# Edge sums with groups dealt out by cost, the look of the next turn ahead, and slice tokens two windows deep

## The reference, cut to what matters

```
x = x + relation_conv(ln(x))        # 8 relations, segment sum over dst
x = x + gat_gated_experts(ln(x))    # attention over 131072 edges gates 4 experts
x = x + sage(ln(x), src, dst)       # below
x = x + slice_attention(ln(x))      # below

# sage
h_sparse = maxk(feat @ W_neigh, 32)
summed = segment_sum(h_sparse[src], dst)
out = feat @ W_self + summed / max(deg, 1)

# slice attention, 8 heads x 64 slices
w = softmax((x_mid @ W_slice + b_slice) / temp)      # per node and head
slice_token = einsum(fx_mid, w) / (w.sum(nodes) + 1e-5)
```

## Time and profile before

| | us |
|---|---|
| median of 3 runs | 5771.85 (5771.05 to 5776.82) |
| the profiled execution | 5768.18 |
| its span | 5766.4 |

### The profile page before, as it was taken

The page is one execution under the profiler, slowest core; times in us unless marked ns, Lnnn a source line. Parts: engine busy times, 40 slices in busy tenths (PEclk is TensorE's granted clock), DMA queues, the critical chain, the costliest instruction groups (busy, mean ns, idle before and its releaser), DMA issues. The chain is left out here.

```text
span 5766.4 us, 72842 instructions
## 1 busy us (share of the span) xinstructions
PE 4709.5 (82%) x18114; PEld 2969.5 (51%) x18115; DVE 2677.6 (46%) x9248; ACT 1130.5 (20%) x2248; POOL 3249.8 (56%) x3351
## 2 busy tenths in 40 slices
PE   3998887888788888824999999957688999984888
PEld 1553333333333333313777777744466788852446
DVE  6562333333333222242555555557866555634442
ACT  1331000000000000002444444434211111100222
POOL 1114777777777777711777777722477766670001
PEclk9997566666666655555999999979899999986998
DMA  3333333333334333312323233342455544431001
GB/s 133 131 124 127 105 105 105 105 105 105 105 105 112 105 105 105 105 29 45 60 59 59 59 59 59 60 143 99 131 161 155 147 132 132 129 107 24 0 0 45
DMA packets 312422, 545.12 MB, mean 95 GB/s; under 512 B 74736, under 2 KB 212735, under 8 KB 305811
## 3 DMA queue, kind: packets, MB, share of 16 engines
q0 software_dynamic: 141088, 319.86, 21.4%
q1 hardware_dynamic: 171092, 222.51, 12.0%
HBM read 449.02 MB, written 93.08 MB: 94 GB/s over the span
## 5 line engine op out<-in xcount | busy, mean ns | idle before, releaser
L959 PE MATMUL e_sums<-e_ring,e_onehot 128*128 128x257 f32 x3136 | 1621.6, 626 | 345.1 <-DMA e_ring<-table,erow 260.5
L713 POOL DMA_INDIRECT e_ring<-table,erow x1568 | 1490.6, 951 | 477.9 <-issue 360.0
L959 PEld LDWEIGHTS e_sums<-e_ring,e_onehot 128*128 128x128 f32 x3136 | 722.5, 281 | 1239.1 <-issue 908.3
L1878 POOL DMA_INDIRECT t_source<-source_rows,t_index x848 | 809.7, 955 | 281.3 <-issue 230.9
L1049 POOL DMA_INDIRECT e_ring<-table,esrc x800 | 789.4, 987 | 311.0 <-PE e_sums L1136 158.0
L914 DVE SCALAR_TENSOR_TENSOR big<-e_sums,within,big 128x257 f32 x196 | 95.0, 485 | 1286.4 <-PE e_sums L959 1286.4
L1136 PE MATMUL e_sums<-e_ring,e_onehot 128*128 128x256 f32 x1600 | 484.2, 411 | 112.2 <-DMA e_ring<-table,esrc 91.8
L1122 PE MATMUL e_total<-e_loads,e_times 128*128 128x256 f32 x2176 | 538.2, 382 | 0.0
L2027 PE MATMUL t_raw<-big,t_w 128*128 (+1 forms) x1600 | 441.3, 438 | 1.3
L1122 PEld LDWEIGHTS e_total<-e_loads,e_times 128*128 128x128 f32 x2176 | 399.7, 191 | 65.2
L1136 PEld LDWEIGHTS e_sums<-e_ring,e_onehot 128*128 128x128 f32 x1600 | 298.9, 199 | 237.0 <-DVE e_onehot L1091 103.6
(11 more groups left out here) (383 smaller groups left out, 5214.8 us busy)
## 6 DMA issues: line engine op xcount, KB each, us to landing
table<-r_stage SPq DMA_DIRECT2D x49, 1024.0 KB
e_loads<-table SPq DMA_DIRECT2D x384, 128.0 KB
t_near<-near_rows SPq DMA_DIRECT2D x106, 256.0 KB
e_ring<-table,erow POOLq DMA_INDIRECT x1568, 2.7
m_outputs<-first_outputs SPq DMA_DIRECT2D x49, 512.0 KB, 4.6
first_outputs<-t_stage SPq DMA_DIRECT2D x96, 256.0 KB
t_source<-source_rows,t_index POOLq DMA_INDIRECT x848, 2.4
e_ring<-table,esrc POOLq DMA_INDIRECT x800, 3.1
```

The lines of the kernel that those rows point to most:

```text
L713: eng.indirect_dma_start(ring[:, t % BODY, 0:D], None, table, bass.IndirectOffsetOnAxis(ap=b.erow[:, t:t + 1], axis=0)).then_inc(gathered[ ...
L959: eng.matmul(sums[g % SUMS][:, 0:ACCW], onehot[t % ONEHOTS][:, :], ring[:, t % BODY, :], start=(t % GROUP == 0), stop=(t % GROUP == GROUP ...
L1878: eng.indirect_dma_start(source[s][:, q, :], None, a.source_rows, bass.IndirectOffsetOnAxis(ap=index[s][:, q:q + 1], axis=0)).then_inc(gat ...
```

## The change

Six things change. **Neighbour sums**: (1) a group's place among the tiles follows from a cost of 3 + 4 x width, dealt over 784 tiles; (2) the row marks are made by ScalarE as Relu(1 - |source - column|), two Abs and one Relu per group, two groups ahead of the copy; (3) the totals lie in two sets of PSUM banks, two windows to a bank, cleared by matmuls with zeros, and a block's totals are taken in after six groups of the next block. **Attention edges**: (4) `look` of turn t+1 stands behind `hide` of turn t, so `columns` is called for two turns in a body. **Slice tokens**: (5) the bias matmul goes; `blogit` is made on all 128 partitions and VectorE adds it, PSUM to SBUF, ahead of the maximum; (6) GpSimd normalises the rows, into four buffers instead of two; turning is parted from scoring and stands two windows ahead; the loop is written out. The diff, cut:

```diff
 neighbour_sums
-    BODIES = (NT - FROM) // BODY
-    BEGIN = [sum(DGROUPS // n for n in DSTEPS[0:i]) for i in range(DENSE + 1)]
+    LATER = 6
+    TILES = NT - FROM
+    GROUPS = DENSE * DGROUPS
+    COST = [3 + 4 * wide(g) for g in range(GROUPS)]
+    tile_of = [sum(COST[0:g]) * (TILES - BODY) // sum(COST) for g in range(GROUPS)]
+    groups_at = [[] for _ in range(TILES)]
+    for g, at in enumerate(tile_of):
+        groups_at[at].append(g)
...
-        row = [sb(f"e2_row{s}", [P, P], BF16) for s in range(MARKS)]
+        zeros = sb("e2_zeros", [P, BANK], BF16)
+        away = [sb(f"e2_away{s}", [P, 2, P]) for s in range(2)]
+        row = [sb(f"e2_row{s}", [P, 2, P], BF16) for s in range(MARKS // 2)]
...
-        total = [ctx.enter_context(nc.psum_tensor(f"e2_total{k}", [P, BANK], F32)) for k in range(DWIDE)]
+        total = [ctx.enter_context(nc.psum_tensor(f"e2_total{s}", [P, DWIDE, D], F32)) for s in range(2)]
...
 scalar
+            def mark(g):
+                s = g % 2
+                wait_if(eng, rowed, g - 1)
+                for two in range(2):
+                    c = column(2 * g + two)
+                    eng.activation(away[s][:, two, :], b.ramp[:, 0:P], ACT.Abs, bias=b.dsrc[:, c:c + 1],
+                                   scale=-1.0).then_inc(parted, 1)
+                wait_if(eng, tallied, g - MARKS // 2 + 1)
+                eng.wait_ge(parted, 2 * (g + 1))
+                eng.activation(row[g % (MARKS // 2)][:, :, :], away[s][:, :, :], ACT.Relu, bias=b.ones[:, 0:1],
+                               scale=-1.0).then_inc(rowed, 1)
...
+            mark(0)
+            mark(1)
+            for g in range(GROUPS):
+                if g + 2 < GROUPS:
+                    mark(g + 2)
+                copy(g)
...
 vector, mark
-                    eng.tensor_scalar(row[q][:, :], rampn[:, :], b.dsrc[:, column(tile):column(tile) + 1], None,
-                                      ALU.is_equal).then_inc(marked, 1)
...
 vector, order
+                for g in groups_at[t]:
+                    mark(g)
+                    if g % DGROUPS == LATER and g > DGROUPS:
+                        take(block(g) - 1)
+                if t % GROUP == 4 and t // GROUP >= 1:
+                    add(t // GROUP - 1)
+            add(TILES // GROUP - 1)
+            take(DENSE - 1)
...
 tensor, inner
+                if g % DGROUPS == 0:
+                    wait_if(eng, taken, BEFORE[max(n - 1, 0)])
+                    for q in range(0, DWINDOWS[n], 2):
+                        eng.matmul(into[:, q:q + 2, :].rearrange("p w d -> p (w d)"), zeros[:, 0:P], zeros[:, :],
+                                   start=True, stop=False, skip_group_check=True)
...
 attention_edges, tensor
             def body(t, s, w, e):
-                column = columns(t)
-                look(t, s, column)
                 if e is not None:
                     hide(t, w, e)
+                if not last_turn(t, 1):
+                    look(t + 1, 1 - s, columns(t + 1))
                 if e is not None and not first_turn(t, 1) or isinstance(t, int) and t == UNITS:
                     project(t - 1, 1 - s, e - 1 if e else EXPERTS - 1)
-                total(t, s, column)
+                total(t, s, columns(t))
...
 slice_weights, tensor
-                eng.matmul(bias[0:1, h * SG:(h + 1) * SG], bx[:, h:h + 1], wslice[:, :], start=True, stop=False)
-                mm = eng.matmul(bias[0:1, h * SG:(h + 1) * SG], one[:, :], bslice[:, :], start=False, stop=True)
+                eng.matmul(bias[:, h * SG:(h + 1) * SG], bx[:, h:h + 1].broadcast_to([SD, P]), wslice[:, :], start=True, stop=False)
+                mm = eng.matmul(bias[:, h * SG:(h + 1) * SG], b.ones[0:1, :], bslice[:, :], start=False, stop=True)
...
 slice_tokens
+        @block.gpsimd
+        def _(eng):
+            for s in range(XNS):
+                eng.memset(xn[s][:, D:ACCW], 1.0).then_inc(ones, 1)
+            for w in range(NW):
+                wait_if(eng, summed, w - XNS + 1)
+                eng.tensor_scalar(xn[w % XNS][:, 0:D], b.x[:, w, :], b.mean[:, w:w + 1], b.rstd[:, w:w + 1],
+                                  ALU.subtract, ALU.mult).then_inc(normed, 1)
...
 vector, lower
-                eng.tensor_reduce(top[s][:, :], by_head(logits[s][:, :]), AX_X, ALU.max).then_inc(topped, 1)
+                eng.tensor_tensor(biased[s][:, :], logits[s][:, :], f.blogit[:, :], ALU.add).then_inc(topped, 1)
+                eng.wait_ge(topped, 2 * w + 1)
+                eng.tensor_reduce(top[s][:, :], by_head(biased[s][:, :]), AX_X, ALU.max).then_inc(topped, 1)
...
 scalar
+            copy(0, 0)
+            copy(1, 1)
+            grow(0, 0)
+            for w in range(NW):
+                if w + 2 < NW:
+                    copy(w + 2, w % 2)
+                keep(w)
+                if w + 1 < NW:
+                    grow(w + 1, (w + 1) % 2)
...
 tensor
-                eng.matmul(logits[s][:, :], b.ones[0:1, :], f.blogit[:, :], start=False, stop=True).then_inc(scored, 1)
...
+            turn(0, 0)
+            turn(1, 1)
             score(0, 0)
+            for w in range(NW):
+                if w + 1 < NW:
+                    score(w + 1, (w + 1) % 2)
+                if w + 2 < NW:
+                    turn(w + 2, w % 2)
+                tokens(w, w % 2, LAST if w == NW - 1 else P)
```

More of the change, by code:

```diff
@@ L1029, in _, with copy @@
             for s in range(AHEAD):
-                eng.wait_ge(fetched[s], 16 * (DENSE * DGROUPS // AHEAD))
-        @block.scalar
+                eng.wait_ge(fetched[s], 16 * (GROUPS // AHEAD))
+        @block_ctx.scalar
         def _(eng):
-            for g in range(DENSE * DGROUPS):
+            def mark(g):
[9 more added lines that the diff above has]
+                               scale=-1.0).then_inc(rowed, 1)
+            def copy(g):
                 n = wide(g) * P
@@ L1038, in _ @@
                 eng.activation(times[g % TIMES][:, 0:n], tally[g % 2][:, 0:n], ACT.Copy).then_inc(copied, 1)
-        @block.gpsimd
+            mark(0)
+            mark(1)
+            for g in range(GROUPS):
+                if g + 2 < GROUPS:
+                    mark(g + 2)
+                copy(g)
+        @block_ctx.gpsimd
         def _(eng):
@@ L1100, in _ @@
-            add(BODIES * BODY // GROUP - 1, 1)
-            eng.wait_ge(added, 2 * (BODIES * BODY // GROUP))
-            eng.wait_ge(taken, BEFORE[DENSE])
-        @block.tensor
+                if a.n:
+                    a.settled()
+                if k.n:
+                    k.settled()
+                for q in range(DWINDOWS[n]):
+                    window = b.accs[:, bass.ds(w + q, 1), 0:D].rearrange("p a c -> p (a c)")
+                    k.did(eng.tensor_tensor(window, window, total[n % 2][:, q, :], ALU.add))
@@ L1107, in outer @@
                 wait_if(eng, copied, g - 1)
+                eng.wait_ge(rowed, g + 1)
+                eng.wait_ge(marked, 2 * (g + 1))
                 for two in range(2):
-                    q = (2 * g + two) % MARKS
-                    eng.wait_ge(marked, 2 * (2 * g + two + 1))
-                    mm = eng.matmul(tally[g % 2][:, 0:wide(g) * P], row[q][:, :], place[q][:, 0:wide(g) * P],
+                    mm = eng.matmul(tally[g % 2][:, 0:wide(g) * P], row[g % (MARKS // 2)][:, two, :],
+                                    place[(2 * g + two) % MARKS][:, 0:wide(g) * P],
                                     start=(two == 0), stop=(two == 1))
@@ L1119, in inner @@
                 eng.wait_ge(copied, g + 1)
                 eng.wait_ge(fetched[g % AHEAD], 16 * (g // AHEAD + 1))
-                for k in range(DWINDOWS[n]):
-                    mm = eng.matmul(total[k][:, 0:D], times[g % TIMES][:, k * P:(k + 1) * P], loads[:, g % AHEAD, :],
-                                    start=(r == 0), stop=(r == DGROUPS - 1))
+                for q in range(DWINDOWS[n]):
+                    mm = eng.matmul(into[:, q, :], times[g % TIMES][:, q * P:(q + 1) * P], loads[:, g % AHEAD, :],
+                                    start=False, stop=False, skip_group_check=True)
@@ L1124, in inner @@
                 mm.then_inc(spread, 1)
[L1126 to L1142 removed]
+            eng.wait_ge(numbered, 2)
@@ new lines, in _ @@
+            for t in range(TILES):
+                s, g8 = t % BODY, t // GROUP
+                if t % GROUP == 0:
+                    wait_if(eng, added, 2 * (g8 - 1))
+                eng.wait_ge(matched, t + 1)
+                eng.wait_ge(gathered[s], 16 * (t // BODY + 1))
+                eng.matmul(sums[g8 % 2][:, 0:D], onehot[t % ONEHOTS][:, :], ring[:, s, :],
+                           start=(t % GROUP == 0), stop=(t % GROUP == GROUP - 1)).then_inc(summed, 1)
+                for g in groups_at[t]:
+                    outer(g)
+                    if g > 1:
+                        inner(g - 2)
+                    if g == GROUPS - 1:
+                        inner(g - 1)
+                        inner(g)
@@ L2056, in _ @@
```

(2 more changed lines are left out.)

172 lines of the change are left out of this document (55 added, 117 removed).

## The result

The changed kernel takes 5589.66 us (median of 4 runs, 5585.27 to 5592.74), the kernel before 5771.76 beside it: a ratio of 0.9682, 95% interval 0.9665 to 0.9699. The forecast was 5598, in a range of 5550 to 5660. The profiled execution took 5587.87 us, its span 5586.1, against 5766.4.

A forecast was written before the change was run, and what follows sets the result against it. GpSimd and, in wide blocks, TensorE bound neighbour sums; GpSimd bounds attention edges; a circle of waits bounds slice tokens. Gains 55 + 8 + 110 = 173 us gave 5598 us, own range 5565 to 5630, with rivals A and B 5550 to 5660.

The forecast's parts named there:

- The dealt groups: Neighbour sums: dealing groups by cost moves the bound from TensorE to GpSimd; gathers 1042 us against 1099, net 55 gained.
- The stretch: Neighbour sums, wide blocks: GpSimd's issue lengthened beside VectorE's wide marks, 0.18 us per group, giving 1.318 us per tile.
- stand closer without the row marks between them: Neighbour sums, a bound: marks of a burst closer together, stretch 0.14 per tile, about 24 us gained.
- Rival A: Neighbour sums: the stretch vanishes with the row marks, GpSimd keeps 1.25 us; 42 us more gained, 5556; chance 0.13.
- rival B: Slice tokens: each window's subtraction or product waits out a whole GpSimd normalisation, 1.22 us; 59 us, so 5657; chance 0.14.
- Row marks on ScalarE: Neighbour sums: two Abs and one Relu per group fit on ScalarE, 1.1 to 1.4 us with the copy; cost taken as nothing.
- Rival D: Neighbour sums: Abs or Relu needs another function table, two loads per group; stage 1410 us, kernel 5966; chance 0.02.
- 8 of the 19 us: Attention edges: the earlier look removes part of GpSimd's waits for VectorE; 8 us taken from a span of 0 to 19.
- rival C: Attention edges: the second column load is not hidden and TensorE's turn grows; 5646; chance 0.09.
- the period 4.6: Slice tokens: a window takes 4.6 us instead of 7.0, from VectorE's chain of 4.58; net 110 gained, bounds 85 to 121.
- TensorE's work was taken as 4.5: Slice tokens: TensorE's own work per window, scores, turning, flips and tokens, 4.5 us together, nearly tying with VectorE's chain.

The follow-up runs named there:

- rows_on_vector: The changed kernel with the row marks of the neighbour sums made by VectorE again, all else kept: 5563.39 us, ratio 0.9639 to the kernel before.
- deep_rows: The changed kernel with row marks back on VectorE and slice tokens' lowering and scoring one window deeper: 5554.3 us, ratio 0.9615 to the kernel before.
- load_twice: The kernel of look_back with the column offsets loaded a second time ahead of the totals: 5608.24 us, ratio 0.9701 to the kernel before.
- look_back: The changed kernel with the look of turn t back ahead of its hidden layer and one offsets load per turn: 5610.16 us, ratio 0.9704.

## Why the prediction was right

**The dealt groups: right in its mechanism.** With the old places the gathers took 1098.4 us, 53 more than the changed kernel's 1045.4. That TensorE stops being the bound and GpSimd is late next is what the idle time before the gathers says.

**The stretch: the size nearly right, and that by luck.** The step "1.25 + 0.18/2.706 = 1.318 us per tile" took the stretch per group from the kernel before. It measured 1.333: 0.084 us a tile where 0.068 was taken, 520 x 0.015 = 8 us more. The narrow blocks, taken at 1.275, ran at 1.258 and 1.264 (3 us less), which takes nearly half of it back. The text tied the stretch to how many wide marks VectorE makes; it depends on how they follow each other. The figure came from a kernel with row marks between the place marks, and rows_on_vector, which deals the same groups with the row marks still there, has 0.029 a tile and not 0.068. The sum took more than twice what its own reason gives, and the marks that then ran into each other, which it left out, made up for that. The one clause that came near, marks that "stand closer without the row marks between them", stood only as a bound. Taking the row marks off VectorE cost 25 us and did not gain.

**Rival A: its time was within reach, for another reason.** It had the stretch vanish with the row marks. It nearly vanished when they came back (0.029), or when waits stood between the marks (0.020).

**The rule named for rival B.** The Trainium skill ("SBUF — State Buffer", section "SBUF: two separate sides") calls the port pair that the two engines share an exclusive lock: whoever begins first has it for the whole instruction, and the other blocks. On the gathers the trace agrees in direction: an issue of 0.95 us took 1.54 beside a run of marks, though the 185 issues under such runs took 1.14 on average. In slice tokens it agrees where VectorE's product began first: the normalisation 0.06 us behind it took 0.51 us more, of the 0.63 that the product had left. It does not agree where the normalisation began first, in deep_rows: the product did not wait for the 0.67 us that were left.

**Row marks on ScalarE, costed at nothing: right, with less cover than said.** Groups from 4092 to 5150, and the timeline in the first block:

```profile
L1040 ACT ACTIVATE e_away<-ramp,dsrc 128x128 f32<-128x128 f32 x768 | 261.5, 391 | 21.0 <-PEq L106 21.0
L1044 ACT ACTIVATE e_row<-e_away,ones 128x256 bf16<-128x256 f32 x384 | 194.9, 508 | 36.7 <-ACT e_away L1040 1.9
```

```profile
4131.61 0.26 ACT L1051 ACTIVATE e_times<-e_tally 128x128 f32<-128x128 f32 x1
4131.77 0.68 ACT L1040 ACTIVATE e_away<-ramp,dsrc 128x128 f32<-128x128 f32 x2
4132.54 0.51 ACT L1044 ACTIVATE e_row<-e_away,ones 128x256 bf16<-128x256 f32 x1
4132.95 0.26 ACT L1051 ACTIVATE e_times<-e_tally 128x128 f32<-128x128 f32 x1
```

A group repeats after 1.34 us on ScalarE, and the gathers bring one every 1.258 x 0.997 = 1.25. ScalarE is the slowest engine of that block, near the upper end of the estimate (1.1 to 1.4). Over 64 groups it falls back by 64 x 0.09 = 6 us, which is less than the 16 x 1.25 = 20 us for which the ring holds gathers, and GpSimd shows no wait. As an estimate from these numbers, a block of width 1 some three times as long would show one; that was not tried.

**Rival D: false.** No table load stands before Abs or Relu in those groups, and the stage took 1055.5 us and not 1410.

**Attention edges: right in direction, 3 us short.** 8 of the 19 us were taken; 11.3 came, and 12 when the look alone was put back. The 19 was too large: 7.4 of it stands ahead of the first gather. Between first and last gather there were 15.2 us beyond the ordinary gaps, of which the changed kernel keeps 5.0, the wait for the first weights. So all that could be won here was won. The second load is hidden, so rival C is false: load_twice against look_back, 0.3 us on the gathers.

**Slice tokens: 10 us short.** The forecast made the period 4.6 out of VectorE's chain of 4.58, and it was 4.40. The chain, start to start: addition 0.72, maximum 0.72, subtraction to exponential 0.72, exponential and hand-over 0.67 are as forecast; sum and reciprocal took 0.96 where 1.04 was taken, and from product to the next addition 0.61 where 0.69 was: the addition does not depend on the product and starts before it ends. That is 0.16 of the missing 0.2, and 48 x 0.2 = 10 us. 4.40 lies below the range's own end of 4.45, which named that overlap as "a little".

TensorE's work was taken as 4.5 and is 4.11 at most, from deep_rows. Start to start, deep_rows shows 1.72 us for the scores, 0.22 for turning and 2.17 for flips and tokens, where 1.91, 0.33 and 2.2 to 2.3 were taken from a window in which TensorE stood idle between its steps. It did not matter for the forecast, only because VectorE's circle was the longer one.

**Rival B: false.** Product and subtraction show 0.692 us, and a doubled normalisation leaves the period at 4.393. Its price is false too: in deep_rows the product begins in the middle of a normalisation and takes 0.69.

## What to carry to other kernels

Where GpSimd issues gathers back to back, look at the mean of one issue against its median. Here the difference was what VectorE took from it, and it followed how VectorE's marks stood to each other and not its busy time. Before moving work off VectorE, ask what stood between its long operations; here a wait between two marks (32 us) was worth more than the move, which cost 25. Add up a chain from start to start and not from durations, and ask of each link whether the next really needs it.

## What the hardware did that was not expected

An indirect gather of 128 rows costs GpSimd 0.946 + 0.305 = 1.25 us undisturbed. Beside place marks that ran into each other single issues took 1.54 us and up to 2.46, most far less; with waits between the same marks none took over 1.21. A VectorE operation with two tiles in SBUF as inputs held an issue up as well, by 0.54 us beside 0.67 us of it. And between a GpSimd normalisation and a VectorE product that starts 0.06 us ahead of it, GpSimd alone was slowed, from 1.22 to 1.73 us; where the product started 0.55 us behind the normalisation, neither was.
